# Gated cross-attention and routed feed-forward on one core: the expert product turned by TensorE, and the drain's queues in another order

## The reference

```python
x = x + tanh(g_xattn) * attention(layernorm(x), ctx)       # 8 groups of 2 heads, self and cross
def moe(x):                                                # x = layernorm(x), 2048 tokens of 256
    scores = softmax(x @ gate_w.T)                         # 8 experts
    topk_w, topk_idx = top_k(scores, 2)
    topk_w = topk_w / sum(topk_w)
    y_all = einsum('eti,eih->eth', silu(x @ w1) * (x @ w3), w2)   # w1, w3: 256 x 176; w2: 176 x 256
    y = sum(y_all[topk_idx, tok] * topk_w)
    return y + silu(x @ sw1) * (x @ sw3) @ sw2             # shared: width 352
x = x + tanh(g_ffn) * moe(layernorm(x))
```

## Time and profile before

| | |
|---|---|
| three runs | 1017.22, 1021.95, 1022.38 us; median 1021.95 |
| the profiled execution | 1025.24 us, its span 1023.4 us |
| TensorE, VectorE, ACT, POOL busy | 84%, 75%, 74%, 72% of the span |
| granted TensorE clock, mean | 0.921 of full speed |
| DMA queues' share of 16 engines | q1 (SP) 36.1%, q0 (POOL) 5.8%, q10 (ACT) 2.4% |
| chain that ended last | PE 60%, DVE 13%, ACT 6%, SP's issues 6%, DMA 5% |

### The profile page before, as it was taken

The page is one execution under the profiler, slowest core; times in us unless marked ns, Lnnn a source line. Parts: engine busy times, 40 slices in busy tenths (PEclk is TensorE's granted clock), DMA queues, the critical chain, the costliest instruction groups (busy, mean ns, idle before and its releaser), DMA issues.

```text
span 1023.4 us, 20701 instructions
## 1 busy us (share of the span) xinstructions
PE 859.8 (84%) x6222; PEld 617.3 (60%) x6222; DVE 765.5 (75%) x1744; ACT 753.4 (74%) x2432; POOL 732.9 (72%) x569
## 2 busy tenths in 40 slices
PE   0475899999999999999999999999876567787493
PEld 0353677777787777777777878777633333343241
DVE  8898888889888898988988888888657744222135
ACT  3486899999999999999999999999663123332220
POOL 4598789799899889889979989988632163334433
PEclk9687899999999999999999999999977778888686
DMA  9323224243333324233333424332643179999533
GB/s 249 103 83 98 63 53 78 53 77 73 62 66 77 72 51 98 51 75 74 66 62 58 90 51 77 72 73 55 155 85 111 57 142 180 189 188 190 130 90 101
DMA packets 251371, 96.66 MB, mean 94 GB/s; under 512 B 227616, under 2 KB 244992, under 8 KB 251328
## 3 DMA queue, kind: packets, MB, share of 16 engines
q1 hardware_dynamic: 236848, 77.78, 36.1%
q0 software_dynamic: 7856, 12.33, 5.8%
q10 hardware_dynamic: 6624, 6.03, 2.4%
HBM read 31.88 MB, written 10.22 MB: 41 GB/s over the span
## 4 chain that ended last, share of the span: by engine, by line
PE 60%; DVE 13%; ACT 6%; SPq 6%; issue 5%; DMA 5%; another core or an unknown queue 3%; POOL 2%; ACTq 0%; DVEq 0%; POOLq 0%
PE S L509 10%; PE A L414 7%; PE A L415 7%; PE T L480 5%; PE JB L539 5%; PE S L497 4%; PE VB L406 3%; DMA psrc<-w_lo 3%; SPq L363 3%; SPq L358 2%; PE VB L408 2%; PE VB L407 2%; PE T L530 2%; DVE stage L1113 1%
## 5 line engine op out<-in xcount | busy, mean ns | idle before, releaser
L1614 POOL TENSOR_TENSOR rstd<-var,mhalf 128x8 f32<-128x8 f32 (+1 forms) x128 | 191.1, 1509 | 64.5 <-DVE var L1191 64.0
L414 PE MATMUL A<-w_hi,xq 128*128 128x256 f16 (+1 forms) x1024 | 187.2, 249 | 34.2 <-DVE v_lo L1165 19.7
L415 PE MATMUL A<-w_lo,xq 128*128 128x256 f16 (+1 forms) x1024 | 187.2, 249 | 0.0
L509 PE MATMUL S<-kT,qT 128*128 128x256 f32 x512 | 144.0, 406 | 11.0 <-ACT kT L870 7.6
L1177 DVE TENSOR_SCALAR qT<-T,qmap 128x512 f32<-128x512 f32 x128 | 103.4, 808 | 60.1 <-PE T L480 60.1
L1149 DVE TENSOR_REDUCE nmx<-S 128x2 f32<-128x512 f32 (+1 forms) x192 | 114.6, 597 | 28.0 <-PE S L509 25.7
L881 ACT ACTIVATE prob<-S,nmx 128x256 f32<-128x256 f32 x256 | 119.6, 484 | 13.8 <-DVE nmx L1149 12.7
L414 PEld LDWEIGHTS A<-w_hi,xq 128*128 128x128 f16 x1024 | 101.4, 99 | 45.3 <-issue 29.0
L1681 POOL TENSOR_TENSOR raw<-raw,rstd 128x1024 f32<-128x1024 f32 x64 | 126.5, 1976 | 0.0
L1665 POOL TENSOR_TENSOR prob<-prob,rl 128x1024 f32<-128x1024 f32 x64 | 121.0, 1891 | 0.0
L509 PEld LDWEIGHTS S<-kT,qT 128*128 128x128 f32 x512 | 91.0, 196 | 47.0 <-ACT kT L870 20.0
(11 more groups left out here) (245 smaller groups left out, 2377.1 us busy)
## 6 DMA issues: line engine op xcount, KB each, us to landing
stage<-wallT SPq DMA_DIRECT2D x8, 1024.0 KB, 5.3
yd<-pT ACTq DMA_DIRECT2D x46, 128.0 KB
wp<-wpT POOLq DMA_DIRECT2D x1, 2048.0 KB, 30.9
zd<-zr SPq DMA_DIRECT2D x8, 256.0 KB, 2.4
out<-xs SPq DMA_DIRECT2D x8, 256.0 KB
xs<-x SPq DMA_DIRECT2D x1, 1792.0 KB, 21.3
pT<-psrc SPq DMA_TRANSPOSE x110, 4.9
raw<-w13T SPq DMA_DIRECT2D x2, 704.0 KB, 4.8
```

The source lines that it names most:

```text
L414: nc.tensor.matmul(o, l, w_hi[:, c, col:col + n], start=(c == 0), stop=False)
L415: last = nc.tensor.matmul(o, l, w_lo[:, c, col:col + n], start=False, stop=(c == HC - 1))
L509: last = nc.tensor.matmul(o[:, t * S:(t + 1) * S], qT[:, p, 0, h, t * P:(t + 1) * P], kT[:, p, 0:S], start=True, stop=True)
L1614: return nc.gpsimd.tensor_tensor(dst, src, mhalf[:, 0:n], ALU.pow)
```

## The change

It does six things.

1. The two halves of the expert product are no longer turned by a DMA transpose on SP, but by TensorE: `turn_a(j)`, four transposes of 128 by 128 in f16 against an f16 identity `idh`, into the two PSUM banks T0 and T1; VectorE copies the result to SBUF (`read_a`). The columns of `ea` beyond 176 are set to zero once (POOL). `expert_down(j)` stands 3 tiles behind `expert_up(j)` instead of 4.
2. The stores of the results go from ACT's queue to SP's, behind `flip_z`.
3. The phases of the routing have 8 and 8 token tiles (four and four batches), 23 and 23 expert tiles. The work of the second phase is spread over more expert tiles, its logits stand ahead of them.
4. In the ticks behind the loop ACT no longer begins with the first cut of weights; attention work stands ahead of it, and the high halves of the last two steps come a tick earlier. SP loads unit 2 ahead of the last flip.
5. POOL issues six gathers of z ahead of `shared_low(3)` to `(5)`, and the gathers of y 0 to 7 in pairs behind the last four gathers of z.
6. Shared pieces 3 to 5 stand behind `pick_tokens(0)` on TensorE; VectorE has two sums (`mix`) ahead of the shared work behind the tiles, and `mix(6)`, `mix(7)` behind the last `finish`.

The diff, cut to what the text speaks of:

```diff
-NE = NT - ST
-NT0, NT1 = ((2 * P * n + E * (P - 1)) // P for n in (NE, ST))
+NE = NT // 2
+NT0, NT1 = ((2 * P * n + E * (P - 1)) // P for n in (NE, NT - NE))
-DL = 4
+DL = 3
...
-        ea = ps_flat[:, 8 * H:8 * H + 3 * 4 * P].rearrange("p (r k n) -> p r k n", r=3, k=2)
+        kt_flat = kT[:, :, :].rearrange("p a k -> p (a k)").bitcast(F16)
+        ea = kt_flat[:, 0:2 * 4 * P].rearrange("p (r k n) -> p r k n", r=2, k=2)
+        idh = flo[:, LG + 6 * 2 * H:LG + 6 * 2 * H + P]
-        at = pt_flat[:, 0:4 * 4 * P].rearrange("p (r k n) -> p r k n", r=4, n=P)
+        at = pt_flat[:, 0:2 * 4 * P].rearrange("p (r k n) -> p r k n", r=2, n=P)
+        turned_a = [t_[:, :].bitcast(F16)[:, 0:4 * P].rearrange("p (k n) -> p k n", n=P) for t_ in (T0, T1)]
...
@@ SP
-            def flip_a(j):
-                done(sp, e_al, j)
-                done(sp, e_dn, j - 4)
-                sp.dma_start_transpose(at[:, j % 4, :, :], ea[:, j % 3, :, :].rearrange("p k n -> p (k n)")).then_inc(ld_at[j % 4], 16)
+            def store_y(j):
+                done(sp, e_y, j)
+                sp.dma_start((yd[0][j * P:(j + 1) * P, :] if j < NT0 else yd[1][(j - NT0) * P:(j - NT0 + 1) * P, :]), yo[:, j % 4, :]).then_inc(st_y[j % 4], 16)
...
-            for n in (STEPS - 2, STEPS - 1):
-                flip(n)
-            for u in range(2, UNITS):
+            flip(STEPS - 2)
+            sp.wait_ge(f_wlo, 1)
+            load_up(2)
+            load_down(2)
+            flip(STEPS - 1)
+            for u in range(3, UNITS):
...
-            for j in range(NTL):
+            for j in range(NTL + DL + 1):
                 if j + 3 < NTL: flip_z(j + 3)
-                flip_a(j)
+                if 0 <= j - DL < NTL: store_y(j - DL)
@@ TensorE
+            def turn_a(j):
+                done(pe, e_al, j)
+                done(pe, e_ev, j - 2)
+                if j == 0:
+                    done(pe, e_id, 0)
+                if j == 1:
+                    done(pe, f_fin, M0 // FS - 1)
+                for k in range(4):
+                    last = nc.tensor.transpose(turned_a[j % 2][:, k, :], ea[:, j % 2, k // 2, k % 2 * P:(k % 2 + 1) * P], idh)
+                last.then_inc(e_at, 1)
...
             def expert_down(j):
-                landed(pe, ld_at, j)
+                done(pe, e_ev, j)
...
+            for m in range(3, M0): shared_up(m)
             for m in range(3, M0): shared_down(m)
+            pe.wait_ge(zr_read, 16 + 32 * B)
+            done(pe, d_x1, B - 1)
+            logits(NE, NT, JB, R_LG - NE * E).then_inc(f_lgm, 1)
             load_expert(0)
             for j in range(NTL + DL):
                 if j < NTL: expert_up(j)
                 if j + 1 < NTL: load_expert(j + 1)
+                if 0 <= j - 2 < NTL: turn_a(j - 2)
                 if j >= DL: expert_down(j - DL)
-                if j == 7: rank(1)
-                if j == 12:
-                    for t in range(NE, NT): table(1, t)
-                if j == 16: pick_tokens(1)
+                if j == 5: rank(1)
+                if j in (9, 11):
+                    for t in range(NE + 2 * (j - 9), NE + 2 * (j - 9) + 4): table(1, t)
+                if j == 14: pick_tokens(1)
@@ ScalarE, first tick behind the loop (g == 0)
-                    if g <= 3: scale_out(n0 - 5, par(5), 1, group(5))
                     if g == 0:
-                        ffn_high(0)
+                        scale_out(n0 - 5, par(5), 1, group(5))
                         high_px(n0 - 3, par(3), 3)
                         high_p(n0 - 3, par(3), 3)
...
                         exp_cross(n0 - 1, par(1))
+                        scale_out(n0 - 4, par(4), 1, group(4))
+                        high_px(n0 - 2, par(2), 2)
+                        high_p(n0 - 2, par(2), 2)
+                        ffn_high(0)
...
             for j in range(NTL + DL):
                 if j < NTL: expert_silu(j)
-                if j >= DL: read_y(j - DL)
+                if j > DL: read_y(j - DL - 1)
                 if j < NTL: high_a(j)
-                if j >= DL: store_y(j - DL)
+            read_y(NTL - 1)
@@ VectorE
+            def read_a(j):
+                done(dve, e_at, j)
+                done(dve, e_dn, j - 2)
+                nc.vector.tensor_copy(at[:, j % 2, :, :], turned_a[j % 2]).then_inc(e_ev, 1)
...
-            for j in range(NTL):
-                expert_mul(j)
-                low_a(j)
+            for j in range(NTL + 2):
+                if j < NTL: expert_mul(j)
+                if j >= 2: read_a(j - 2)
+                if j < NTL: low_a(j)
...
-                if j == 9:
-                    count_tiles(1)
-                    for t in range(NE, NT): marks(t)
+                if j == 7: count_tiles(1)
+                if 7 <= j <= 10:
+                    for t in range(NE + 2 * (j - 7), NE + 2 * (j - 6)): marks(t)
...
+                if j == 16: read_tokens(1)
@@ GpSimd
+            for j in range(6): fetch_z(j)
             for m in range(3, M0): shared_low(m)
-            for j in range(NTL):
+            for j in range(6, NTL):
                 fetch_z(j)
                 if j == 16: exps(1, NE, NT)
-            for i in range(2 * NT): fetch_y(i)
+                if j >= NTL - 4:
+                    for i in range(2): fetch_y(2 * (j - NTL + 4) + i)
+            for i in range(8, 2 * NT): fetch_y(i)
```

More of the change, by code:

```diff
@@ L251, in build @@
         ld_zt = [sem("ld_zt%d" % k) for k in range(4)]
-        ld_at = [sem("ld_at%d" % k) for k in range(4)]
         st_y = [sem("st_y%d" % k) for k in range(4)]
@@ L612, in shared_up @@
                 if m == 0:
-                    done(pe, a_q1, STEPS - 1)
+                    done(pe, d_v, STEPS - 1)
                     done(pe, f_lgr, 0)
@@ L713, in expert_down @@
                     wh, wl = (w[0:n, bass.ds(e * (2 * H) + k * H, H)] for w in (w2_hi, w2_lo))
-                    ah, al = (at[0:n, j % 4, 2 * i + k, :] for i in range(2))
+                    ah, al = (at[0:n, j % 2, 2 * i + k, :] for i in range(2))
                     last = split3(o, ah, al, wh, wl, start=(k == 0), stop=(k == 1))
@@ L719, in _ @@
                 tick(B, g)
[L720 to L723, removed]
+            for t in range(4): table(0, t)
             shared_down(0)
-            shared_up(3)
             for t in range(4, 8): table(0, t)
             shared_down(1)
-            shared_up(4)
-            for t in range(8, 12): table(0, t)
+            for t in range(8, NE): table(0, t)
+            pick_tokens(0)
             shared_down(2)
-            shared_up(5)
-            for t in range(12, NE): table(0, t)
-            pick_tokens(0)
+            for m in range(3, M0): shared_up(m)
             for m in range(3, M0): shared_down(m)
+            pe.wait_ge(zr_read, 16 + 32 * B)
+            done(pe, d_x1, B - 1)
+            logits(NE, NT, JB, R_LG - NE * E).then_inc(f_lgm, 1)
             load_expert(0)
@@ L1004, in high_a @@
                 done(act, e_a, j)
-                landed(act, ld_at, j - 3)
-                nc.scalar.activation(ea[:, j % 3, 0, 0:I], ap[:, j % 2, :], ACT.Copy).then_inc(e_ah, 1)
+                done(act, e_at, j - 2)
+                if j == 0:
+                    done(act, e_pad, 0)
+                nc.scalar.activation(ea[:, j % 2, 0, 0:I], ap[:, j % 2, :], ACT.Copy).then_inc(e_ah, 1)
             def read_y(j):
@@ L1011, in read_y @@
                 nc.scalar.activation(yo[:, j % 4, :], (A0, A1)[j % 2][:, 0:H], ACT.Copy).then_inc(e_y, 1)
-            def store_y(j):
-                done(act, e_y, j)
-                act.dma_start((yd[0][j * P:(j + 1) * P, :] if j < NT0 else yd[1][(j - NT0) * P:(j - NT0 + 1) * P, :]), yo[:, j % 4, :]).then_inc(st_y[j % 4], 16)
             for g in range(LAGS):
                 tick(B, g)
-            ffn_high(2)
-            shared_silu(3)
-            shared_high(3)
             ffn_high(3)
             tail_high(B - 1)
-            shared_silu(4)
-            shared_high(4)
-            shared_silu(5)
-            shared_high(5)
             ffn_high(4)
+            for m in range(3, M0):
+                shared_silu(m)
+                shared_high(m)
             for j in range(NTL + DL):
                 if j < NTL: expert_silu(j)
-                if j >= DL: read_y(j - DL)
+                if j > DL: read_y(j - DL - 1)
                 if j < NTL: high_a(j)
-                if j >= DL: store_y(j - DL)
+            read_y(NTL - 1)
             for m in range(M0, MS):
@@ L1526, in mix @@
             def mix(q):
+                done(dve, f_fin, 2 * q // BT)
                 dve.wait_ge(ld_yk[q % (NG // 4)], 64 * (q // (NG // 4) + 1))
@@ L1605, in _ @@
             shared_low(M0 + 5)
-            mix(4)
             finish(3)
-            for q in range(5, NT // 2): mix(q)
+            for q in range(6, NT // 2): mix(q)
         @block.gpsimd
@@ L1735, in fetch_z @@
                     done(pool, f_idx, j // NT0)
-                    pool.wait_ge(zr_read, 16 + 32 * (B - 1 + j // NT0))
```

(3 more changed lines are left out.)

120 lines of the change are left out of this document (55 added, 65 removed).

## The result

The change takes 988.31 us (median of 4 runs, 986.38 to 992.21) where the kernel before takes 1022.16 (4 runs): a ratio of 0.9686, 95% interval 0.965 to 0.972, or 33.9 us less. The forecast was 976 us in a range of 952 to 1004, so the sign and the range held and 12 us of the gain did not come. Its profiled execution has a span of 986.0 us against 1023.4.

The account below looks back on a forecast made before the run. DMA engines and SP's queue together were taken to set the tile period. Terms -20 + 6 - 2 - 8 - 20 - 2 = -46 us on the profiled 1025.2 gave 979, forecast 976 us for the median, range 952 to 1004.

Parts of the forecast that it names:

- Ahead of the loop, -20 us: Stage before the expert tiles: weight cut moved, fewer routing marks, earlier gathers; -20 us, bounds -8 and -30.
- Part (a): Ahead of the expert loop: ACT's weight cut moves behind the last steps' softmax work, removing its load wait; -8 us.
- Parts (b) and (c): Ahead of the expert loop: fewer marks and narrower plan, -7.7 us; six earlier gathers, -6, with 2 charged for delayed low halves.
- The period of a tile: Expert loop: period falls from 2.78 to 2.35 us, bounds 2.05 and 2.8; -20 us over 46 tiles.
- T = (3.5 + L)/3: Expert loop: SP's in-order store and flip set tile period T; flip landing L taken as 3.5 us gives 2.33 us.
- rival 2: Expert loop: TensorE's floor sets the tile at 2.1 us and the gathers' stall goes whole; 957 us, chance 0.18.
- Routing in the loop, +6 us: First 19 expert tiles: the larger second routing phase on VectorE delays multiplies; +6 us, bounds 0 and 13.
- The gathers, -8 us: End of expert loop: rearranging sixteen gathers of y removes half of a 15 us stall; -8 us, bounds 0 and -15.
- Behind the loop, -2 us: After the expert tiles: two sums instead of three behind the last finish, gather issue under shared products; -2 us.
- rival 4: Expert stage: TensorE's clock stays at the lower level, tile 4.0 us; 1052 us, chance 0.05.
- rival 3: Expert loop: tile 23's gather waits for late second-phase routing, TensorE stands 10 to 15 us; 988 us, chance 0.12.
- theories A, A1 and A2: Experiments' explanations of TensorE's gap: gathers themselves; back-to-back gathers; every gather however spaced, losing 15 to 20 us in pieces.

Follow-up runs that it names:

- the third sitting: Third group of runs, kernel before 1003.98 us: unedited change 959.55 us, beside all gathers behind the loop, stores on ScalarE, and those stores with gathers spread.
- the second sitting: Second group of runs, kernel before 1025.5 us: unedited change 990.44 us, beside versions with the turn undone, turns doubled, and ScalarE's first weight cut moved back.
- the first two sittings: First two groups of runs, each kernel compared with the kernel before in its own group, which took 1003.72 and 1025.5 us.
- the first experiment: Against the change, all 32 gathers of y moved behind the last store of the loop: 971.37 us, ratio 0.9686 to the kernel before.

## Why the prediction was right, and where its steps failed

**Ahead of the loop, -20 us: right.** 21.5 us in the first profile (106 to 84.5), and TensorE's first up-product at 806.46 where I said near 808. Part (a), booked at 8, measured 8.0 in the median when undone alone, 10.6 at the first product. Parts (b) and (c) were not tried apart; they are what is left.

**The period of a tile: nearly the right size, a wrong reason.** I forecast 2.78 to 2.35; the steady tiles went from 2.68 to 2.285 in the first profile and to about 2.21 in both later ones. The step that failed is "T = (3.5 + L)/3", SP's order as the bound. With the stores taken off SP the steady tile stayed (2.195 and 2.225, against 2.19 to 2.215 with them on it). The densest tiles are set by TensorE: twelve matmuls of 1.76 us and turns of 0.23, together 1.99 us, against 2.01 measured. I had priced the turns at 0.35 and put that floor at 2.1. So rival 2's mechanism held, with 0.2 us of small waits a tile on it, whose cause no run takes apart. SP's order costs something only where landings are long, in the burst: 2.7 us in the loop, by the profiles of the third sitting.

What the turn bought is shown by undoing it: the DMA share back to 1.00 and SP's flips back to back, the tile back to 2.695, as the first part of the prediction read it from the earlier trace rows. It came to 11.4 us in all, and 13.3 between first and last product, not 20: the 20 steady tiles give 9.6 of it, the 12 ahead 1.4 and the 13 behind, with the gap in both, 2.3. As the undone version had its stores on ScalarE, which went with 6 us in the other place, the turn alone may be worth up to 17, an estimate from 11.4 and 6.1.

**Routing in the loop, +6 us: too much.** Products 0 to 12 took 31.3 us in the first profile, 12 steady tiles of 2.285 are 27.4, which leaves 3.9 for routing and the pipeline's filling. Before, the same reckoning leaves 3.4 (35.5 less 12 of 2.68). So the wider second phase shows 0.5 us more there than the old one, within the bounds of 0 to 13. The copy's price was the other one: the estimate of some 0.4 us, from the table in the Trainium skill (VectorE: DVE Perf Modes, "The perf-mode tier table"), fits its 0.415, my 0.7 does not.

**The gathers, -8 us: this is the term that failed.** "The cause is not in the trace; I take half of it as gone." In the forecast's profile the stall did not shrink, it grew. The six tiles from product 34 to product 40 took 37.7 us where six steady ones take 13.7: 24.0 lost, where I had booked 15 before and 7 after. In the second sitting it is 32.0 for 13.3, 18.7 lost; in both the tail has its own wait of 8.9 us. In the third sitting there was little of it: the same six tiles took 16.1. There the change gains 44.4 us, close to the sum's 46, but by luck: the sum had 8 in it for a stall that the change does not show in that place, and that before, at 1004 us, can hardly have had there. Against its own execution the sum said -46 us, and the two profiled executions, 1025.24 and 987.78, are 37.5 apart, a miss of 8.5. It is a balance: the expert stage is 13 us short of its sum (some 17 by the gathers and 2 by the period, against 5.5 by the routing), the other two stages are 4.4 over.

**Behind the loop, -2 us:** 4.9 in the first profile. **The clock** (rival 4) stayed at 0.97 in the undisturbed stage of the first profile and was 0.81 in the 30 us around the gap in the second sitting. It fell behind waits and did not stay down; single tiles behind a wait were stretched by it, as the spread gathers show. Whether the turns count as busy for it no run here shows. **The second phase late** (rival 3) did not happen: product 23 follows 22 by 2.1 us (862.2, 864.4).

**What stays open.** What holds TensorE's completions back in the burst, and whether its work or only the signal comes late. Shown: it goes with the place (or the sitting) the program ran in and not with the stores' queue (the undone turn has it with the stores on ScalarE; the change itself lacks it in the third sitting). Not shown: what differs between the places; the first two sittings even bear the same chip number. Nor did a version without a burst run where the stall is, so whether spreading the gathers, or moving them behind the loop, cures it there is untested, and theories A, A1 and A2 are not decided. Nor is it told which of the two full resources, SP's queue or the DMA engines, the turn relieved.

## What to carry to other kernels

When the DMA engines and the queue that issues flips are full, as here, moving one transfer a tile onto TensorE can pay even if TensorE then becomes the bound. Its new floor is read by adding the inserted instructions' start-to-start distance to the old run of matmuls. Keep the queue that issues the input transfers free of what waits for a result: a store that waits for the tail of the pipeline delayed the flips, which cost nothing in the steady tiles and 2.7 us where a landing took 6.3. And a stall whose releaser the trace does not name gets its full length as the likeliest value, with a look at whether the kernel before even shows it in another sitting.

## What the runs showed that I had not expected

In the gap, TensorE's work is on record long before anyone sees its result. In the second sitting its last turn is recorded at 917.54, and from there to 925.88 TensorE, VectorE and ScalarE start nothing, while POOL goes on issuing:

```profile
917.54 0.39 PE L717 MATMUL T<-w_lo,kT 128*128 128x128 f16 x4
925.88 0.32 ACT L1011 ACTIVATE prob<-S 128x176 f32<-128x176 f32 x1 [10.28 <-remote]
```

ACT's silu waits for an up-product whose last matmul was issued at 913.55, 12.3 us earlier. The transfers don't explain it by their mass: in the first profile, the fourteen microseconds from 906 to 920 hold one queue at 38.5 per cent, no block of instructions, flips or stores among them:

```profile
DMA packets 540, 1.49 MB, mean 107 GB/s; under 512 B 176, under 2 KB 176, under 8 KB 540
## 3 DMA queue, kind: packets, MB, share of 16 engines
q0 software_dynamic: 540, 1.49, 38.5%
```

It ends with the burst: 1.7 us after the last gather's issue ends in the first profile (918.95, 920.63), 2.4 in the second sitting (923.46, 925.88). It is not tied to the gathers of y either: in the first profile tile 0's last up-product matmul is recorded at 807.21 and its silu starts at 809.92, beside gathers of z; in the first experiment the two stand at 806.64 and 806.99. Between the second and the third sitting the kernel before differs by 21.5 us and the change by 30.9, more than most edits to either; in the profiles of the change 17.6 of 23.0 us lie between first and last product, where the gap is.
